# Nine of the 21 returned key rows are loaded during the last tile of the first phase

## The reference

```python
xn = _layernorm(x)
# relational message passing
transformed = einsum('ni,rio->rno', xn, weight)          # 16 relations
gnn = segment_sum(transformed[rel_type, src] * norm, dst)
# linear attention with a gate, over all nodes
q, k, v = split(xn @ Wqkv);  k = softmax(k, axis=nodes)
context = einsum('bnhd,bnhv->bhdv', k, v)                # needs every node's key
mix = (q @ context) * sigmoid(gelu(LN(xn) @ Wg1 + bg1) @ Wg2 + bg2) @ Wproj + bproj
x = x + gnn + mix
# eight experts, two chosen per node
x = x + moe(_layernorm(x), router_w, w1, b1, w2, b2)
```

## Time and profile before

| | us |
|---|---|
| median of 3 runs | 1596.96 (1595.99 to 1597.08) |
| the profiled execution's own time | 1598.54 |
| its span | 1596.7 |
| PE busy | 1563.8 (98%) |
| DVE busy | 1339.1 (84%) |
| mean granted clock | 0.995 |

### The profile page before, as it was taken

The page is one execution under the profiler, slowest core; times in us unless marked ns, Lnnn a source line. Parts: engine busy times, 40 slices in busy tenths (PEclk is TensorE's granted clock), DMA queues, the critical chain, the costliest instruction groups (busy, mean ns, idle before and its releaser), DMA issues.

```text
span 1596.7 us, 31746 instructions
## 1 busy us (share of the span) xinstructions
PE 1563.8 (98%) x10509; PEld 1439.2 (90%) x10509; DVE 1339.1 (84%) x3389; ACT 962.8 (60%) x2156; POOL 1021.2 (64%) x1111
## 2 busy tenths in 40 slices
PE   7999999999999999998799999999999999999998
PEld 6888788888888888887699999999999999999998
DVE  7888656488888888884699999999999999999985
ACT  4455322356565665654677776777677777777764
POOL 4433222677777777757687777777777777767720
PEclk9999999999999999999999999999999999999999
DMA  9776665688888889889433333343333333333320
GB/s 301 264 256 242 243 237 226 231 291 272 277 278 279 283 283 284 277 261 317 144 111 108 116 109 108 112 113 104 103 117 107 110 106 109 112 105 113 107 53 10
DMA packets 127076, 290.50 MB, mean 182 GB/s; under 512 B 21271, under 2 KB 49724, under 8 KB 126914
## 3 DMA queue, kind: packets, MB, share of 16 engines
q1 hardware_dynamic: 86068, 177.19, 30.2%
q0 software_dynamic: 39952, 110.13, 26.3%
q10 hardware_dynamic: 894, 1.16, 0.2%
HBM read 149.49 MB, written 138.90 MB: 181 GB/s over the span
## 4 chain that ended last, share of the span: by engine, by line
PE 94%; DMA 1%; DVE 1%; issue 1%; ACT 1%; POOL 1%; ACTq 0%; SPq 0%; DVEq 0%; POOLq 0%
PE bank L1826 74%; PE bank L2030 4%; PE bank L2031 3%; PE bank L1870 2%; PE bank L1871 2%; PE bank L1982 1%; PE bank L1881 1%; PE bank L2026 1%; POOL raw L700 1%; DMA raw<-table,idxa 1%; PE bank L2068 1%; PE bank L2080 1%; PE bank L1836 1%; DMA pad<-in_L_mix_Wg 1%; PE bank L2077 1%
## 5 line engine op out<-in xcount | busy, mean ns | idle before, releaser
L818 POOL DMA_INDIRECT stg<-table,idxcur x495 | 546.7, 1104 | 145.1 <-issue 133.1
L1826 PE MATMUL bank<-wreg,xt 128*128 128x512 f32 x2352 | 579.1, 397 | 0.2
L1826 PEld LDWEIGHTS bank<-wreg,xt 128*128 128x128 f32 x2352 | 433.4, 189 | 88.0 <-ACT stg L864 1.0
L700 POOL DMA_INDIRECT raw<-table,idxa x297 | 306.6, 1032 | 87.7 <-issue 73.7
L1826 PE MATMUL bank<-tt,wreg 128*128 128x256 f32 (+1 forms) x2400 | 324.4, 284 | 0.0
L1826 PE MATMUL bank<-wreg,ht 128*128 128x256 f32 x2352 | 313.1, 282 | 0.2 <-DVE ht L1727 0.2
L1826 PEld LDWEIGHTS bank<-tt,wreg 128*128 128x128 f32 x2400 | 300.4, 189 | 2.5
L1826 PEld LDWEIGHTS bank<-wreg,ht 128*128 128x128 f32 x2352 | 292.1, 189 | 0.4 <-DVE ht L1727 0.4
L1090 ACT ACTIVATE raw<-bank,cols 128x256 f32<-128x256 f32 (+1 forms) x400 | 164.8, 463 | 101.4 <-PE bank L1826 101.0
L1611 DVE SCALAR_TENSOR_TENSOR ml<-stg,nrm,mh 128x256 fp32r<-128x256 f32 x455 | 195.2, 478 | 13.0 <-ACT mh L1034 13.0
L1034 ACT ACTIVATE mh<-stg,nrm 128x256 fp32r<-128x256 f32 x455 | 200.8, 499 | 0.0
(11 more groups left out here) (244 smaller groups left out, 2134.8 us busy)
## 6 DMA issues: line engine op xcount, KB each, us to landing
table<-stg SPq DMA_DIRECT2D x196, 512.0 KB, 3.9
kv_d<-kvs SPq DMA_DIRECT2D x49, 256.5 KB, 5.2
xt_d<-xt SPq DMA_DIRECT2D x49, 256.0 KB, 4.7
xtp<-xt_d SPq DMA_DIRECT2D x24, 512.0 KB
stg<-table,idxcur POOLq DMA_INDIRECT x495
sk<-kv_d SPq DMA_DIRECT2D x24, 256.5 KB, 5.7
out_x<-xres SPq DMA_DIRECT2D x24, 256.0 KB
xres<-in_x POOLq DMA_DIRECT2D x23, 256.0 KB, 4.2
```

What stands on the lines that cost most here:

```text
L700: pool.indirect_dma_start(ring_a[:, r * EARLY + j, :], None, table[0:LIMIT, :], bass.IndirectOffsetOnAxis(ap=idxa[:, at:at + 1], axis=0)). ...
L818: pool.indirect_dma_start(stg[:, ring_at(S, j), :], None, table, bass.IndirectOffsetOnAxis(ap=idxcur[:, at:at + 1], axis=0)).then_inc(gath ...
L1826: mm = pe.matmul(dst, stat(a, c), mov(b, c), start=(n == 0), stop=(n == 3 * chunks - 1))
```

## The change

Group 0 goes into the front of `later` instead of `slot`, group 1 into `slot`, group 2 into the second half of `later`. The seven rows of group 0 lie within the first 3591 numbers of `wreg`, the place of the weights of j = 0 and 1; these are free once the last tile's second relation product is done (`gnn_mm` at 8k + 2). SP issues these seven loads inside the last tile's `stores`, ahead of all four `table` pieces. Two rows of group 1 are issued after the second `table` piece, when the last early sum is done (`sum_a`). The other 12 rows follow the last `table` piece as before.

```diff
+    FREE_ROWS, NEAR_ROWS = 5, 2
@@ rows_of
-            return slot if g == 0 else later[:, SLOTS * (g - 1):SLOTS * g]
+            return slot if g == 1 else later[:, SLOTS * (g // 2):SLOTS * (g // 2 + 1)]
@@ stores, behind the kv_d store
+                if at(k, NT - 1):
+                    for b2 in range(2):
+                        sp.wait_ge(kv_st[b2], 16 * ((NT - HELD + 1 - b2) // 2))
+                    sp.wait_ge(gnn_mm, 8 * k + 2)
+                    load_rows(0, 0, 4)
+                    load_rows(1, 4, SLOTS)
                 for h in range(PIECES):
@@ behind the table piece h
+                    if at(k, NT - 1) and h == 1:
+                        sp.wait_ge(sum_a, ER)
+                        load_rows(2, 0, NEAR_ROWS)
+            def load_rows(part, first, last):
+                for n in range(first, last):
+                    sp.dma_start(rows_of(part)[:, n, :], kv_d[group(group_of(part))[n]]).then_inc(kv_in[part], 16)
@@ behind the last tile's stores
-            sp.wait_ge(sum_a, ER)
-            sp.wait_ge(kv_st[0], 16 * (NP + 1))
-            sp.wait_ge(kv_st[1], 16 * NP)
-            load_rows(0)
-            load_rows(1)
+            load_rows(2, NEAR_ROWS, 4)
+            load_rows(3, 4, FREE_ROWS)
+            sp.wait_ge(ctx1_mm, KEPT)
+            load_rows(3, FREE_ROWS, SLOTS)
+            sp.wait_ge(gnn_mm, 8 * NT)
+            load_rows(4, 0, 4)
+            load_rows(5, *span_of(5))
             first_phase_over(sp)
-            for part in range(2, 2 * GROUPS):
-                load_rows(part)
```

## The result

The changed kernel takes 1601.4 us, the median of 19 runs (1597.13 to 1606.72), against 1597.48 for the kernel before on the same chip (19 runs, 1594.5 to 1604.08). The ratio is 1.0027, 95% interval 1.0016 to 1.0037. It is slower by 3.9 us where 0.6 us of gain were forecast, and it lies above the range.

What follows compares the result with a forecast made beforehand. PE, busy 98% of the span, was taken as the bound. A 3.5 us gain less 2.1 us of gather delay left 1.4, half clock cut it to 0.6: 1596.96 to 1596.4 us, range 1593.0 to 1598.3.

Steps and rivals of the forecast that it cites:

- (b): SP's queue: nine early loads leave a 2.1 to 2.8 us backlog before the last `table` piece; gathers 2.1 us late.
- (e): Remaining effects, costed at nothing: earlier rows and experts' weights, GpSimd 2 us later, added SP waits.
- (a): Early loads of parts 0 and 1: PE's contexts run 726.6 to 732.7 against 738.94 before, front end gives 6 us.
- (c): Gathers to group 3's sums: these end at 745.82 plus gather delay, against 749.32; gain 1.4 us at full clock.
- (d): PE's 3.8 us wait before the first sums brings half clock until some 741.6, cutting the gain to 0.6 us.
- the yardstick: End of PE's sums of gather group 3, 749.32 before, forecast 748.75; what it moves by, the program moves by.
- The forecast of T0: Issue of the last `table` piece: SP loses little, seven load issues taking 3.82 us, 709.9 to 713.7.
- the third: Rival: `table` pieces land late, gathers about 5.2 us late; 1.7 us slower, up to 3.3 with half clock; chance 0.13.
- turning points: Gather delay at which the change turns slower: 3.5 us, or 2.7 us with the half clock.
- The rule of the Trainium skill: DMA queues: each engine consumes one ring's descriptors in order and takes turns between rings; said to speak against the change.

Runs made afterwards that it cites:

- e6: Changed kernel with GpSimd's preparation, DVE's shifts and ACT's exponentials of parts 0 and 1 ahead of their waits; no ratio stated, PE waited 5.67 us for the first message.
- e1: Changed kernel's buffer places, but all 21 row loads behind the last `table` piece; equals the kernel before, no ratio stated.
- e13: Changed kernel plus 12 matrix products that nobody reads, between the contexts of part 1 and the first sums; 1.0035 of the kernel before.
- e4: Changed kernel with the last tile's `hg_d` store issued on ACT's queue instead of SP's; 1.0025 of the kernel before.
- e9: Changed kernel with contexts of parts 2 and 3 also ahead of the first gather group's sums; 1.0038 of the kernel before, five runs.
- e15: Changed kernel with the experts' weight loads held back until the first edge sums are done; 1.0008 of the kernel before.
- e3: Changed kernel with GpSimd's preparation ahead of its wait for the `hg_d` and `kv_d` stores; 1.0011 of the kernel before.
- e14: Changed kernel with only seven early loads and GpSimd's preparation ahead of its waits; 1.0010 of the kernel before.
- e10: Changed kernel with contexts of parts 0 to 3 ahead of the first sums and GpSimd's preparation ahead of its waits; 1.0029 of the kernel before, six runs.
- e5: Changed kernel with only five early row loads, four behind the second `table` piece, one behind the third; 0.19% slower than the kernel before, eleven runs.
- e8: Changed kernel with five early loads behind the second and third pieces, and GpSimd's, DVE's and ACT's preparations ahead of their waits; no time or ratio stated.
- e18: Changed kernel with only part 0's four row loads early, ahead of the first piece; 0.9983 or 0.9982 of the kernel before (text doesn't assign which).
- e16: Changed kernel with only part 0's four rows early and GpSimd's preparation ahead of its waits; interval 0.9971 to 0.9993 of the kernel before.

## Why the prediction was wrong, point by point

The step that failed is the sentence at the end of (b): "The landing of `hg_d` ... moves by about the same". From it I let the gathers start late by the backlog of the last piece, d = 2.1. In fact `hg_d` landed 4.2 us later, GpSimd's preparation came out behind it, and the gathers started 4.7 us later. A second step failed beside it, "The rest at nothing" of (e): from first gather to first message it took 10.6 us, not 9.0.

- **(a) the front end** was sized at 6 us. The rows were early, but the shift stood behind `hg_d` as GpSimd does. From T0, the contexts start at 7.9 where the forecast had 5.7. Its size mattered little: e6 delivers it entirely, PE starts without a wait, and the gathers take it back.
- **(b) the backlog of the piece** was right in size for this execution, 2.6 us within the stated 2.1 to 2.8, and 1.9 to 4.7 over the profiles with nine early loads. The way to it was not: the 3.8 us of idle DMA time were read up to 722, behind the issue of both stores. Up to `hg_d`'s issue and up to the last piece's the kernel before had:

```profile
713.00:719.99 6.99, 6.99 (x36) 5.76 (x36) 4.32 (x11) 3.26 (x6) 0.00 (x0) 1.00 0.67 259
713.00:720.92 7.92, 7.75 (x38) 6.14 (x38) 5.09 (x13) 3.26 (x6) 0.00 (x0) 1.00 0.60 232
```

  That is 2.3 us idle ahead of `hg_d` and 3.2 ahead of the piece (3.1 and 3.9 in e1's profile). `hg_d` stands ahead of an almost idle microsecond (share 0.10), so it has 0.8 us less room than the piece, and 5.9 - 2.3 = 3.6 us of delay would have been the estimate for it. It landed 4.2 us later than before, not 2.1, and GpSimd's preparation of 3.6 us, in before 1.9 us inside the wait for the piece, came out behind it. G grew by 4.7: 4.2 for the landing and 1.7 for the longer preparation, less the 1.2 that were free. I had named `hg_d` as what starts GpSimd, and not laid its chain (landing, preparation, gather) beside the piece's. With the earlier trace rows it can be done: preparation begins at 721.91, the first gather at 725.00 after 1.23 us of waiting, so only 1.23 us of lateness were free on this path.
- **(c) from gather to message** I assumed unchanged, 8.97 us. It was 10.6: another 1.7 us (0.2 to 1.7 over e13, e4, e9 and this profile). e15 gives 2.7 back by holding the weights. This is the step of (e) "the rest at nothing" that failed too: loads that move up do not have to be wanted by anyone to hurt. It is enough to take the gain away: e3 and e14 have gathers late by just 2.1 us, and boundaries of 29.7 and 31.2, where a gain of 0.6 would be 28.5; M is 10.3 and 10.1 in them.
- **(d) the clock** was right in kind and size. PE had a wait ahead of the first sums, and the half clock behind it. From the first sums to the yardstick I had 12.25 us (736.5 to 748.75); it took 754.32 - 741.91 = 12.4. The first sums were to start at T0 + 15.6 and started at T0 + 20.1. These 4.5 us are 2.6 for the gather's start (4.7 - 2.1), 1.7 for the message and 0.2 from the message to the sums. With 0.2 behind them it makes the 4.7 us between a gain of 0.6 and a loss of 4.1.
- **The forecast of T0** held: it moved by 0.88 with the whole first phase, and SP lost nothing.

Of the rivals, the third (table pieces late enough to lose) had the right sign and nearly the right size (1.7 to 3.3 us), and in this profile the wrong path: the piece was 2.6 us late, and it was `hg_d` and what stands behind it that made 4.7. In e10 and e13 the piece itself was 4.7 and 4.1 us late, so its path exists as well. Its turning points, 3.5 us or 2.7 with the half clock, lay too high: e3 and e14 are not faster at 2.1. The rule of the Trainium skill that I had put beside (b) (DMA: Bandwidth & Descriptors, Queues, rings and completion order) agrees with a piece that lands 2.6 us later behind row loads on its own queue. By its turns between rings one could expect `hg_d` on ACT's queue to be early; the 5.59 us of e4 against 5.75 say that it wasn't.

The account that the runs show is in the main a matter of quantity. The idle DMA time was 2.3 us ahead of `hg_d` and 3.2 ahead of the last piece (3.1 and 3.9 in e1). Four rows need 1.05 MB / 400 GB/s = 2.6 us; they about fit, delay nothing that can be read and give 0.17%. Seven need 4.6 and nine 5.9; the surplus stands in front of the last stores, and the ratio goes to 1.0014 and 1.0027. Place counts too: e5's five rows need 3.3 us, but stand nearer to `hg_d`, and lose.

Open: whether the second phase's half clock explains e5 and e8 in all their runs as it does in e5's profile. And the clock's part: the mean clock of the changed kernel's runs is 0.9936, that is 0.0064 x 2 x 1601 = 20.5 us at 1.2 GHz in each, some 4 us more than before. In the two profiles the low stretch at the boundary is of like length in both kernels, and what the changed kernel has more lies at 783 to 790. Whether it has that stretch more often than the kernel before, and how much of the 3.9 us is due to it, one profile of each can't tell.

## What to carry to other kernels

Before moving loads up, measure the idle DMA time between their new place and the issue of the next store or load that someone waits for, and not beyond that issue, and move no more bytes than fit in it: here four loads gained 0.17% where seven and nine lost. Look at every transfer in the stretch, the small ones that only a barrier waits for above all, and write the whole chain behind each landing beside the one that you watch. Read such distances from more than one execution: here the same nine loads delayed the same piece by 1.9 to 4.7 us. Work that needs nothing from a barrier belongs ahead of it, but it pays only where its engine is late.

## What the runs showed of the hardware

- A store, `hg_d`, that lands in under 1.9 us on engines with idle time takes 5.75 us on full ones (DMA share 1.03), and 5.59 us from another engine's queue.
- GpSimd waits beside DVE. Its `affine_select` on 128x256 took 0.46 us in e3 and 0.67 in e18, and 1.51 in the changed kernel, where DVE did its two shifts from 727.37 to 729.72, one after the other, so the first until about 728.55. The select ended at 728.92, 0.4 us behind that; the second one ended at 730.03, 0.3 us behind the second shift. The Trainium skill (SBUF — State Buffer, SBUF: two separate sides) states that a DVE instruction with two SBUF inputs and a GpSimd one that reads SBUF lock the shared ports against each other for a whole instruction; these rows agree.
- PE's granted clock stayed at 1.00 behind waits of 2.40 us (changed kernel, 728 to 735) and 1.88 us (e18), and fell behind 5.84 us. But it fell also behind 1.84 us (e3, 0.66 on the mean of 724 to 729) and 1.80 us (e16, 0.72 from 724 to 730), where the 28 products of parts 0 and 1 took 8.02 us instead of 6.34. So the length of the wait just before does not decide it alone.
- The same instructions took 38.2 or up to 40.7 us, from part 4's contexts to the sums behind the 2.63 us wait, in different executions, with the granted clock at 0.51 in the changed kernel's (783 to 790) and at 0.96 before (780 to 787).
